# Token layers: how pair 0's packed rows are fetched in the first layer, and where the later layers' projections are loaded

## What is computed

```python
x = embed[src] + _pos_encoding(s, D)
for i in range(N):                                  # 4 layers, H = 8 heads of DK = 16
    q, k, v = (x @ W[i] + b[i]).reshape(b, s, H, DK).transpose(0, 2, 1, 3)
    scores = jnp.einsum('bhqd,bhkd->bhqk', q, k) * scale
    ...                                             # softmax, times v, Wo, two layer norms, feed-forward
```

## Time and profile before

| | us |
|---|---|
| median of 3 runs | 1069.77 |
| lowest and highest | 1068.83, 1070.18 |
| the profiled execution | 1067.87 |
| its span | 1066.1 |
| TensorE busy in it | 957.7 (90%) |
| mean granted TensorE clock | 0.94 of full speed |

### The profile page before, as it was taken

One profiled execution on the slowest core, in us unless ns is written; L12 is line 12 of the kernel. 1 busy time (PEld: TensorE's weight loads), 2 busy tenths in 40 slices (PEclk: granted clock), 3 DMA queues, 4 the chain that ended last, 5 costly groups with the idle time before them and its releaser, 6 DMA issues. The chain is left out here.

```text
span 1066.1 us, 20335 instructions
## 1 busy us (share of the span) xinstructions
PE 957.7 (90%) x6977; PEld 684.6 (64%) x6977; DVE 642.7 (60%) x1840; ACT 592.9 (56%) x1333; POOL 407.3 (38%) x612
## 2 busy tenths in 40 slices
PE   3489999999999999873898899997999999987898
PEld 1156666666666666541587666676788888875564
DVE  4467676676766666238436184426577777784773
ACT  4166676676766775524634654416555555543576
POOL 6425677767777775535513000013000010046210
PEclk9589999999999999886789899998999999996999
DMA  4945444544464453001100161100200020007841
GB/s 126 194 102 132 106 97 102 135 97 97 97 149 98 111 111 59 5 1 34 49 2 1 32 203 37 44 1 1 43 11 11 11 72 1 2 20 178 189 83 38
DMA packets 55740, 76.83 MB, mean 72 GB/s; under 512 B 9661, under 2 KB 46823, under 8 KB 51695
## 3 DMA queue, kind: packets, MB, share of 16 engines
q1 hardware_dynamic: 54486, 72.39, 28.8%
q0 software_dynamic: 1152, 3.15, 1.4%
HBM read 53.79 MB, written 17.79 MB: 67 GB/s over the span
## 5 line engine op out<-in xcount | busy, mean ns | idle before, releaser
L2396 DVE TENSOR_REDUCE t_nmax<-banks 128x2 f32<-128x512 f32 x256 | 166.2, 684 | 78.2 <-PE banks L2203 66.3
L2325 ACT ACTIVATE t_probs<-banks 128x512 f32<-128x512 f32 x256 | 144.9, 592 | 81.0 <-PE banks L2225 79.8
L2203 PE MATMUL banks<-t_packed 96*128 96x256 bf16 x512 | 92.7, 282 | 9.7 <-DMA t_packed<-t_qk_pairs 8.7
L2225 PE MATMUL banks<-t_packed 120*128 120x256 bf16 x512 | 92.6, 279 | 9.5 <-DMA t_packed<-t_mT 9.0
L2503 POOL TENSOR_SCALAR xhat<-t_rbuf,mv,rstd 128x128 f32<-128x128 f32 x120 | 94.2, 798 | 3.2
L2203 PEld LDWEIGHTS banks<-t_packed 96*128 96x128 bf16 x512 | 47.3, 100 | 50.0 <-issue 26.3
L2225 PEld LDWEIGHTS banks<-t_packed 120*128 120x128 bf16 x512 | 46.5, 99 | 48.4 <-issue 21.3
L957 ACT ACTIVATE hid<-banks,b 128x344 f32<-128x344 f32 x96 | 51.2, 546 | 45.4 <-PE banks L844 43.3
L1014 DVE TENSOR_TENSOR hid<-hid,every_gate 128x344 f32<-128x344 f32 x96 | 49.7, 555 | 42.5 <-ACT hid L957 28.6
L1322 ACT ACTIVATE l_probs<-banks,l_shift 128x256 f32<-128x256 f32 x128 | 59.5, 473 | 27.8 <-DVE l_shift L1365 25.1
L2238 PE MATMUL banks<-t_probs,t_v 128*32 128x256 f32 x1024 | 73.0, 390 | 0.6 <-ACT t_probs L2325 0.6
(11 more groups left out here) (406 smaller groups left out, 2067.1 us busy)
## 6 DMA issues: line engine op xcount, KB each, us to landing
t_qk_pairs<-t_parts SPq DMA_DIRECT2D x32, 384.0 KB
t_packed<-t_qk_pairs SPq DMA_DIRECT2D x32, 384.0 KB, 5.4
t_packed<-t_qk_pairs SPq DMA_DIRECT2D x32, 256.0 KB, 6.1
every_gate<-gate_rows SPq DMA_DIRECT2D x8, 516.0 KB, 4.9
t_packed<-t_qk_pairs SPq DMA_DIRECT2D x32, 128.0 KB, 6.8
w<-in_L_ffn_w SPq DMA_DIRECT2D x16, 256.0 KB, 2.8
t_packed<-t_mT SPq DMA_DIRECT2D x32, 96.0 KB
g_qk_pairs<-g_parts SPq DMA_DIRECT2D x8, 384.0 KB, 4.8
```

Source lines behind the costliest of these rows:

```text
L2203: ins = pe.matmul(m.mbank[:, n % 3, i * S:(i + 1) * S], m.packed[0:MROW, 0, p, h, c + qt * P:c + (qt + 1) * P], m.packed[0:MROW, 1, p, h, ...
L2225: ins = pe.matmul(scores, m.packed[0:TROW, 1, p, h, c + kt * P:c + (kt + 1) * P], m.packed[0:TROW, 0, p, h, c:c + S], start=True, stop=True)
L2325: act.activation(m.probs[:, n % 6, :], m.sbank[:, n % 2, :], ACT.Exp).then_inc(sem["probs_ready"], 1)
L2396: dve.tensor_reduce(m.nmax[:, b, u // 4, 2 * hp:2 * hp + 2], m.mbank[:, n % 3, :].rearrange("p (i k) -> p i k", i=2), AX.X, ALU.max, negat ...
```

## The change

Pair 0 of layer 0 is read back in halves, one batch at a time: `load_first` issues three DMAs for one batch of queries or keys, each to the same partitions as before but with 8 runs of 512 bytes a partition in place of one of 8 KB. Queries of batch 0 are issued when their store has landed; when the keys' store has landed come the keys of batch 0, then queries and keys of batch 1. Batch 0 counts on a semaphore of its own, for which `M0.0` waits; `M1.0` waits for the rest. All other layer pairs are loaded as before. The projections of layers 1 to 3 are issued behind `x1` of pair 0.

```diff
+        def load_first(k, b):
+
+            for row, part, parts in ((0, 0, 3), (3, 0 if k else 1, 2), (5, 0 if k else 2, 1)):
+                sp.dma_start(m.packed[row * DK:(row + parts) * DK, k, 0, :, b * S:(b + 1) * S],
+                             m.scratch[k, 0, part:part + parts, :, b * S:(b + 1) * S].rearrange("a (d h) n -> (a d) h n", h=H)
+                             ).then_inc(sem["packed"][0] if b else sem["packed_first"], 16)
+
         def load(k, g):
 
             sp.wait_ge(sem["keys_stored"] if k else sem["parts_stored"], 16 * (g + 1))
+            if g == 0:
+                load_first(k, 0)
+                if k:
+                    load_first(0, 1)
+                    load_first(1, 1)
+                return
...
                 load(0 if step == "lq" else 1, g)
-                if (step, g) == ("lk", 1):
-                    sp.dma_start(*w.projections(t, 1, LAYERS - 1)).then_inc(sem["w_proj"], 16)
...
                              m.mT[0:3 * H, b, :].unsqueeze(1).broadcast_to([3 * H, H, S])).then_inc(sem["mrow"][b], 16)
+                if (step, g) == ("x1", 0):
+                    sp.dma_start(*w.projections(t, 1, LAYERS - 1)).then_inc(sem["w_proj"], 16)
...
-                if b == 0 and u == 0:
+                if g == 0 and b == 0 and u == 0:
+                    pe.wait_ge(sem["packed_first"], 16 * 6)
+                elif u == 0 and (b == 1 if g == 0 else b == 0):
                     pe.wait_ge(sem["packed"][p], 16 * 6 * (l + 1))
```

More of the change, by code:

```diff
@@ L1893, in counters @@
     return {name: made[i] for name, i in place.items()}, range(first, last + 1)
-LAYER_SEMS = ("i_ids i_ident i_positions i_cols i_weights i_ids_ready i_ordered i_dve i_sum i_bias w_proj w_rest w_vec w_bc w_rows lin_ready0 lin_ready1 q_ready second_part split_done parts_stored keys_stored rest_ready w_ordered packed0 packed1 packed2 packed3 "
+LAYER_SEMS = ("i_ids i_ident i_positions i_cols i_weights i_ids_ready i_ordered i_dve i_sum i_bias w_proj w_rest w_vec w_bc w_rows lin_ready0 lin_ready1 q_ready second_part split_done parts_stored keys_stored rest_ready w_ordered packed0 packed1 packed2 packed3 packed_first "
               "v_ready max_scores max_taken mparts_done mrow_sb mstored mrow0 mrow1 scores_ready probs_ready av_done o_copied "
@@ L2159, in _ @@
         sp.wait_ge(sem["rows_kept"], 16)
+        sp.wait_ge(sem["packed_first"], 16 * 6)
     @block.tensor
```

## The result

| | before | changed |
|---|---|---|
| median, 18 runs each in turn (us) | 1069.44 | 1066.30 |
| lowest and highest | 1067.28, 1072.54 | 1062.60, 1068.80 |
| the profiled execution | 1067.87 | 1066.7 |
| its span | 1066.1 | 1064.9 |
| mean granted TensorE clock | 0.94 | 0.943 |

The medians differ by 3.1 us. The ratio, taken from runs side by side, is 0.9961, with a 95% interval of 0.9951 to 0.9971: 3.1 to 5.2 us faster, where 2.5 were forecast. The forecast of 1067.3 us was 1.0 us above the measured 1066.3.

A forecast was written before the change was run, and what follows sets the result against it. It took TensorE, idle early in layer 0 while x0 waits on SP's queue behind pair 1's loads and the projections, as the bound; -2.5 us and otherwise zero terms took 1069.8 to 1067.3 us, range 1064.6 to 1070.7.

The forecast's parts named there:

- The projections in front of x0: On SP's queue, 768 KB ahead of x0 take 2.5 us; moving them starts S0.0 at 50.5: -2.5 us.
- The halves as slack: Pair 0's halves start M0.0 some 4.2 us earlier, but x0 still waits behind pair 1's loads until about 48: 0.
- The price of the small runs: Pair 0's loads in 512-byte runs might take 2.3 us longer or 1.3 us less than 8.5; taken as 0.
- the estimate given ahead: By the Trainium skill's page, pair 0's loads in 512-byte runs would be some 17% longer, +1.5 us, giving 1068.8 us.
- SP's own time: Six more issues at 0.44 us end at about 31.2, before pair 1's first store at 32.30: 0.
- The second cover: If SP's issues took 0.99 us each, they would delay stores whose data can't move before 35 anyway: up to +1.
- The projections' new place: Issued behind x1 at 57.3, the projections land at 61, before GpSimd needs them at 63.0: 0.
- The slower rival: The projections land late, at 69.0, and delay GpSimd's Mp0 of pair 1: 2.9 us slower, 1072.7; chance 0.08.
- Two sums of the text: ScalarE's copy ends at 40.4; late projections make the kernel slower from about 8 us between issue and landing.
- Does the gain last: Steps behind S0.0 depend on each other, so the later timeline shifts by the same 2.5 us, the clock perhaps excepted.
- the 0.9 that the forecast gave for the clock: If TensorE's clock still rose at 56.8, 0.9 us of the 2.5 would be given back: 1068.2.
- The forecast's sign of being wrong: Among the signs: the shift of 2.5 us at S0.0 is not found at the end of the timeline.

The follow-up runs named there:

- e2: The changed kernel with the projections put back ahead of x0, so only the halves differ from the kernel before: ratio 0.9987 to the kernel before.
- e10: e2 with the 768 KB of the projections loaded a second time in front of x0: 1069.57 us, ratio 1.0004 to the kernel before.
- e1: The kernel before with only the projections moved behind x1, pair 0 still fetched whole: 1065.28 us, ratio 0.995 to the kernel before.
- e3: The changed kernel with x0 issued ahead of the load of pair 1's keys: ratios 0.9925 and, run again, 0.9964 to the kernel before.
- e9: The changed kernel run once more, unaltered: 1065.28 us, ratio 0.9977 to the kernel before.
- e6: e5 with x0 also ahead of the load of pair 1's queries: 1060.75 us, ratio 0.9947 to the kernel before.
- e5: e3 with pair 2's token steps moved behind S0.3 and GpSimd's batch 1 split ahead of its pair 2 work: 1064.38 us, ratio 0.9966 to before.

## Why the prediction was right

**The projections in front of x0, -2.5 us: right.** e2 and e10 put 2.2 and 2.5 us on one load of 768 KB, and e1 against before, both counted from the issue of pair 1's loads, puts 2.5 on it; e1 alone has the whole gain in time. `S0.0` of the change moved by 2.8: 2.2 of it from the queue and 0.6 from pair 1's loads, issued that much earlier. The 2.5 of its second profile agree by luck, since another wait set them.

**The halves as slack, 0: right in time, as far as the medians can tell, and the reason was named**: pair 1's loads in front of x0 (189 GB/s from 39.3 to 48.4). But the sentence "only if these were gone would the 4 us show" was too simple. In e3 half of them are gone and still the halves show nothing, because the tokens of pair 2 are next.

**The price of the small runs, between -1.3 and +2.3, taken as 0: the sign was a little off.** Pair 1's loads were issued 0.6 us earlier than before, and 1.7 us earlier than in e1, and the halves moved at 180 and 210 GB/s, never the 109 of the broadcast. The guess that the limit is the few partitions written is borne out so far as the size of the run made no loss; it isn't proved. A rival that no run tests is the pace of SP's issues: 1.57 MB in twelve issues of 0.65 us are by this estimate 201 GB/s, about what the loads reached (194), and the DMA share beside them was 0.71, where the 8-KB loads had 0.96 and more. By the rule of the Trainium skill on small descriptors (page DMA: Bandwidth & Descriptors, section Bandwidth) the loads should have been some 17% longer, the estimate given ahead. The trace disagrees: from 26.8 to 34.7 the halves moved at 194 GB/s, the 8-KB loads at 185 from 26.4 to 34.7.

**SP's own time, 0: the cover did not hold.** The twelve issues took 7.83 us, 0.65 each and not 0.44, and pair 1's first store was issued at 33.52, where 32.30 was to hold. The second cover that the text had named, data that can't move before 35, held only in part: the stores' data did begin to move at 34.7, as before, but at 32.8 to 33.4 the queue ran thin (a DMA share of 0.39), so SP's issues may have held up the last loads. It cost nothing that shows at pair 1's loads, which were issued earlier than before.

**The projections' new place, 0: right.** 4.7 us from issue to landing in place of 11.7, `WP` without a wait. The slower rival fell with that.

**Two sums of the text are off, and nothing hangs on them.** ScalarE's copy was to end at 40.2 by its own terms, not 40.4 (it ended at 40.18), and the late projections would have won back the 2.5 us from 8.8 us of landing time on, not 8.

**Does the gain last: this is where the size went wrong, and where luck comes in.** Of 2.8 us at `S0.0`, 1.9 were left at pair 1's maxima (58.78 before, 56.89 after), the 0.9 that the forecast gave for the clock. TensorE's timeline at pair 1's maxima, at `S0.0` of the last pair and in the wide attention, of before:

```profile
58.78 0.60 PE L2203 MATMUL banks<-t_packed 96*128 96x256 bf16 x4
...
439.00 0.99 PE L2225 MATMUL banks<-t_packed 120*128 120x256 bf16 x4 [0.89 <-DMA t_packed<-t_mT]
...
762.51 1.06 PE L1275 MATMUL banks<-vp,l_pT 128*128 128x128 f32 x8
```

and of the change:

```profile
56.89 0.60 PE L2219 MATMUL banks<-t_packed 96*128 96x256 bf16 x4
...
435.79 0.61 PE L2241 MATMUL banks<-t_packed 120*128 120x256 bf16 x4 [0.91 <-DMA t_packed<-t_mT]
...
761.59 1.06 PE L1275 MATMUL banks<-vp,l_pT 128*128 128x128 f32 x8
```

Between them, in the first layer, ScalarE's exponentials have one wait of 3.00 us for TensorE in each of these profiles; of before and of the change:

```profile
125.12 0.60 ACT L2325 ACTIVATE t_probs<-banks 128x512 f32<-128x512 f32 x1 [3.00 <-PE banks L2225]
...
121.47 0.60 ACT L2341 ACTIVATE t_probs<-banks 128x512 f32<-128x512 f32 x1 [3.00 <-PE banks L2241]
```

How many us each profile is ahead of before's at these places:

| profile | `S0.0` | pair 1's maxima | 125 us | last pair's `S0.0` | wide attention |
|---|---|---|---|---|---|
| the change | 2.8 | 1.9 | 3.7 | 3.2 | 0.9 |
| the change again, e9 | 2.5 | 0.7 | 2.4 | 1.2 | 1.9 |
| e1, projections only | 1.4 | 0.9 | 1.6 | 0.3 | 2.1 |
| e2, halves only | 0.6 | 0.3 | 1.1 | 0.4 | 0.1 |
| e10, the weights twice | -1.9 | -2.8 | -1.6 | -4.3 | -7.1 |

From pair 1's maxima to 125 us both profiles of the change won another 1.7 to 1.8 us, and both lack the low stretch at 73.9; e1 and e2, which have one at 74, won 0.7 and 0.8. At 125 us e1's 1.6 and e2's 1.1 add up to 2.7, so by the places the halves have a share, which the medians can't show. In the wide attention only 0.9 are left of the first profile's gain, behind the stretch of 729 to 749 with its lower clock, and 1.9 of the second's. So the "-2.5" is right at `S0.0`, and its sign holds wherever the two profiles of the change were read, but the size does not stay: it moved between 0.7 and 3.7 us. The forecast's sign of being wrong, a shift at `S0.0` that is not found at the end, is met in part, and that the whole came near 2.5 is in part luck. Whether the measured 3.1 to 5.2 us has a steady part above the 2.5, as from the faster loads (0.3 to 0.6 us) or from the clock, stays open: the second measurement, 0.2 to 4.7, holds 2.5, the first does not.

The lowest medians are e3's and e6's, but that either order beats the change isn't shown: e3's second measurement, 0.9964, is that of the change (0.9961), and e6's interval overlaps e9's. e3's edit is one line. In e3 the next wait is 1.81 us for GpSimd, which issues four gathers before it splits the maxima of batch 1.

## What to carry to other kernels

Before splitting a transfer to start its reader earlier, follow the reader's result to the next transfer and ask what is ahead of that one on the queue; here 4.7 us won at the first wait were spent at the second, and a load that nobody needed for 20 us stood in front of the third; moving it gave, alone, all the gain that the medians could tell. Put a load behind the last small transfer that somebody waits for, and check what doubling it costs. Where a change is worth 2 us in 1000, judge it at its place in the trace, and the whole by many executions, more than once.

## What was not expected of the hardware

- Runs of 512 bytes to 48, 32 and 16 partitions moved at 180 and 210 GB/s (the second profile of the change has 191 and 218 in the same stretches) with a DMA share of 0.71 to 0.88, runs of 8 KB to the same partitions at 166 to 196 with 0.93 and more, in two profiles.
- SP's issue of such a 512-byte load took 0.60 to 0.67 us, from the first of the twelve to the last and whatever its size (64 to 192 KB), 0.34 to 0.42 for an 8-KB one in the same place before. No run tells whether the shape or the number of runs costs it.
- The gathers of pair 2, issued at 33 to 39 us in all profiles, let the tokens' sum start at 45.53 in the kernel before and at 46.12 and 48.34 in two executions of the change: beside the big loads their landing varied by 2.2 us from one execution of a kernel to the next.
- After a wait TensorE stayed at 1.2 GHz through 3.6 us of work in e3 and through 9.9 us, 9.4 of them busy, in e5, and one kernel's later low stretches differ between executions.
